# Retention layer of a two-block decoder: the spread of the rotated queries over the heads, from VectorE to ACT

## What is computed

```
x = x + retention(layernorm(x))
def retention(x):
    Q = einsum('bsd,hud->bshu', x, WQ); K = ... WK; V = ... WV
    Q = xpos_rotate(Q); K = xpos_rotate(K)
    QK = einsum('bihd,bjhd->bhij', Q, K)
    scale = 1.0 - 2.0 ** (-5.0 - arange(h))
    R = einsum('bhij,bjhd->bihd', QK * decay_mask(s, scale)[None], V)
    R = group_norm(R, gamma, beta, h)
    return R @ WO
```

## Time and profile before

| what | value |
|---|---|
| median of three runs | 1850.32 us (1847.09 to 1853.89) |
| the profiled execution | 1854.5 us, its span 1852.7 us |
| mean granted TensorE clock | 0.914 of 2.4 GHz |
| TensorE matmuls busy | 1577.7 us, 85% |
| TensorE weight loads busy | 1173.6 us, 63% |
| VectorE busy | 1172.9 us, 63% |
| ACT busy | 714.4 us, 39% |
| POOL busy | 562.4 us, 30% |
| the spread, all layers (L1492) | 640 instructions, 175.6 us |

### The profile page before, as it was taken

One profiled execution on the slowest core, in us unless ns is written; L12 is line 12 of the kernel. 1 busy time (PEld: TensorE's weight loads), 2 busy tenths in 40 slices (PEclk: granted clock), 3 DMA queues, 4 the chain that ended last, 5 costly groups with the idle time before them and its releaser, 6 DMA issues.

```text
span 1852.7 us, 33113 instructions
## 1 busy us (share of the span) xinstructions
PE 1577.7 (85%) x10736; PEld 1173.6 (63%) x10736; DVE 1172.9 (63%) x2970; ACT 714.4 (39%) x1531; POOL 562.4 (30%) x766
## 2 busy tenths in 40 slices
PE   5999949979999999968899995588889999877970
PEld 4655628956666666657799995355556666666850
DVE  5888874357778888775412212677777777775423
ACT  3555555435555555544122220111115555432420
POOL 3111133044443111020133331355551111235526
PEclk9999969989999999959999998798989999776985
DMA  4000000010000000020389894200000000012984
GB/s 170 2 0 0 1 23 23 1 38 10 11 8 4 1 0 0 1 80 1 122 316 328 327 329 167 76 1 0 0 7 13 9 11 9 9 55 86 363 220 136
DMA packets 46683, 137.01 MB, mean 74 GB/s; under 512 B 6445, under 2 KB 29118, under 8 KB 40448
## 3 DMA queue, kind: packets, MB, share of 16 engines
q1 hardware_dynamic: 32288, 110.05, 16.7%
q0 software_dynamic: 7536, 19.67, 3.5%
q10 hardware_dynamic: 6768, 6.16, 1.0%
HBM read 119.21 MB, written 17.56 MB: 74 GB/s over the span
## 4 chain that ended last, share of the span: by engine, by line
PE 57%; DVE 20%; issue 8%; DMA 6%; ACT 4%; POOL 4%; DVEq 1%; ACTq 0%; POOLq 0%; SPq 0%
PE ps L773 9%; PE ps L941 8%; PE ps L818 8%; PE ps L1060 8%; PE ps L851 4%; DVE negmax L1448 4%; PE ps L843 4%; PE ps L1072 4%; DMA back_of<-w_odd 3%; PE ps L866 3%; PE ps L830 2%; DVE probs_all L1456 2%; DVE probsT_all L1443 2%; PE ps L771 2%; PE ps L874 1%
## 5 line engine op out<-in xcount | busy, mean ns | idle before, releaser
L773 PE MATMUL ps<-km,qk 128*128 128x512 f32 x640 | 318.0, 599 | 4.3 <-DVE km L1492 4.3
L1131 ACT ACTIVATE probs_all<-probs_all 128x512 f32<-128x512 f32 x256 | 161.4, 630 | 189.4 <-DVE probs_all L1456 189.4
L1060 PE MATMUL ps<-hT,w_tile 128*128 128x128 f32 x1624 | 203.7, 282 | 3.0 <-DMA w_tile<-in_w_f 2.3
L1448 DVE TENSOR_REDUCE negmax<-ps 128x4 f32<-128x512 f32 x256 | 174.4, 681 | 49.1 <-PE ps L773 48.0
L1060 PEld LDWEIGHTS ps<-hT,w_tile 128*128 128x128 f32 x1624 | 195.6, 198 | 4.4 <-DMA w_tile<-in_w_f 2.5
L638 POOL TENSOR_SCALAR eps_sum<-mv 128x1 f32<-128x1 f32 x112 | 25.0, 223 | 546.0 <-DVE mv L1388 508.0
L1456 DVE TENSOR_TENSOR probs_all<-ps,negmax 128x512 f32<-128x512 f32 x256 | 177.0, 691 | 19.2 <-DVE negmax L1448 1.4
L1492 DVE TENSOR_SCALAR km<-qk,const 128x256 f32<-128x256 f32 x640 | 175.6, 348 | 18.2 <-POOL qk L659 15.6
L773 PEld LDWEIGHTS ps<-km,qk 128*128 128x128 f32 x640 | 119.5, 193 | 83.9 <-issue 73.3
L851 PE MATMUL ps<-const,probs_all 128*128 128x128 f32 x1024 | 160.8, 280 | 12.7 <-ACT probs_all L1131 12.4
L1124 ACT ACTIVATE probsT_all<-ps 128x512 f32<-128x512 f32 x256 | 148.3, 593 | 7.0 <-PE ps L851 6.7
(11 more groups left out here) (240 smaller groups left out, 3104.5 us busy)
## 6 DMA issues: line engine op xcount, KB each, us to landing
w_tile<-in_w_f SPq DMA_DIRECT2D x39, 1536.0 KB, 9.1
w_tile<-in_w_f SPq DMA_DIRECT2D x47, 385.0 KB, 6.1
back_of<-w_odd ACTq DMA_DIRECT2D x47, 128.0 KB
ctxT<-in_ctxT SPq DMA_DIRECT2D x32, 128.0 KB, 2.1
rows_of<-row_of SPq DMA_DIRECT2D x8, 512.0 KB, 3.7
y_back<-back_of SPq DMA_DIRECT2D x8, 512.0 KB, 4.9
w_even<-in_w_att SPq DMA_DIRECT2D x3, 1024.0 KB, 6.9
w_raw<-in_w_f SPq DMA_DIRECT2D x2, 1026.0 KB, 5.5
```

The source lines that it names most:

```text
L773: mm(ps[:, g, :], qk[:, p, stationary + c, :], km[:, c, j:j + HB, :].rearrange("p h k -> p (h k)"), start=mask is None, stop=True).then_in ...
L1060: last = mm(ps[:, 2 * which + at.two, fc * P:(fc + 1) * P], w[:, col:col + P], rowT[:, at.two, c, :], start=c == 0, stop=c == KC - 1)
L1131: nc.scalar.activation(probs[:, g], probs[:, g], ACT.Exp, scale=HD ** -0.5).then_inc(S["probs"], 1)
L1448: nc.vector.tensor_reduce(m, bank, AX.X, ALU.max, negate=True).then_inc(S["dve_sm"], 1)
```

## The change

RET's spread goes to ACT: `spread_queries` issues eight ACTIVATEs (`copy` with a scale: Identity, scale = column j of the head mask, bias 0) into the same `km`, waits for the same POOL semaphore and the same scores, and increments the same km_sb. It is called for `at[1]` ahead of the late `turn_out(at[-1])` and of `weighed(now)`. VectorE's `keys` returns at once for a tile of RET; its wait for POOL stays for the other layer with a rotation.

```diff
--- before.py
+++ after.py
@@ -1173,6 +1173,14 @@
                         last = copy(qk[:, p, m], ps[:, B_QK, m * P:(m + 1) * P], None, vec(names[m // KC], m % KC))
                 last.then_inc(S["qk_sb"], 1)
 
+            def spread_queries(tile):
+
+                wait(act, "pool_m", tile, 3)
+                wait(act, "scores_out", tile.back(1))
+                for j in range(HC):
+                    last = copy(km[:, :, j, :], qk[:, tile.p, 0:KC], head_mask[:, j:j + 1])
+                last.then_inc(S["km_sb"], 1)
+
             def turned_probs(tile, g):
                 if tile.l != RET:
                     last = tile.back(1)
@@ -1209,6 +1217,8 @@
                     exp_zero_keys(now)
                     turned_probs(now, 2)
                     turned_probs(now, 3)
+                if 1 in at and at[1].l == RET:
+                    spread_queries(at[1])
                 if late:
                     turn_out(at[-1])
                 if now:
@@ -1483,11 +1493,13 @@
 
             def keys(tile):
 
+                if tile.l == RET:
+                    return
                 if tile.l in ROTARY:
                     wait(dve, "pool_m", tile, 3)
                 wait(dve, "qk_sb", tile)
                 wait(dve, "scores_out", tile.back(1))
-                src = qk[:, tile.p, 0:KC] if tile.l == RET else qk[:, tile.p, KC:2 * KC]
+                src = qk[:, tile.p, KC:2 * KC]
                 for j in range(HC):
                     last = ts(km[:, :, j, :], src, head_mask[:, j:j + 1], None, ALU.mult)
                 last.then_inc(S["km_sb"], 1)
```

## The result

The changed kernel takes 1916.8 us (median of 4 runs, 1911.6 to 1919.9), the kernel before 1850.7 (4 runs); the ratio is 1.0358, 95% interval 1.0336 to 1.0380. That is 66 us more, where 60 were forecast. The profiled execution took 1918.0 us (span 1916.0) against 1854.5 (1852.7), 63.3 us of span.

A forecast was written before the change was run, and what follows sets the result against it. The order of waits on a loop through TensorE, VectorE and ACT's oT was taken to bind, no engine being full. Delay 52.6, clock 6.5, filling 1 and relief 0 made 60 us on 1850.3: 1910 us, range 1890 to 1932.

The forecast's parts named there:

- The loop and the place of oT: Retention steps: ACT's turned output oT is on the loop that sets the step; VectorE's spread is off it.
- The price of the run: ACT's eight ACTIVATEs: 0.513 us each, starts 0.40 us apart, 3.2 us until ACT's next instruction.
- The cheap end: Rival on ACT: scale operand costs nothing or starts lie 0.26 to 0.31 us apart; 1888 to 1900 us, chance 0.15.
- The delay: ACT's queue: oT waits behind POOL's rotation and the run, 3.76 us later in each of 14 steps, 52.6 us.
- The clock: TensorE's longer wait makes every step a long one: 4 x 1.62 = 6.5 us more.
- The dear case: Rival on TensorE: the 1.2 GHz level covers most of what follows the longer wait; 1926 to 1934 us, chance 0.17.
- Filling: First tiles of retention, filling and draining: ACT's longer run costs 1 us, between 0 and 4.
- VectorE's relief: Taking 2.19 us a step off VectorE is worth nothing; rival that VectorE binds: 31 us gain, 1819 us, chance 0.03.
- The median: Whole kernel: 60 us on top of the median of 1850.3, so 1910 us.
- The other signs: Profile after: steps near 17.8 us, VectorE idle some 6.4 us more, ACTIVATEs 0.40 apart, out projection's wait near 4.7.

The follow-up runs named there:

- filled kernels: TensorE's waits in a retention step filled with unread matmuls: changed kernel (3 and 20) 1892.7 us, ratio 1.0237; kernel before (3 and 3) 1834.4 us, ratio 0.9926.
- one ACTIVATE: Changed kernel, but from the second retention tile ACT issues only one of the eight spreading ACTIVATEs, in the same place: 1867.0 us, ratio 1.0085.
- with four: Changed kernel, but ACT spreads four heads ahead of the turned output and VectorE the other four where it used to: 1897.1 us, ratio 1.0268.
- with sixteen: Changed kernel, but ACT issues eight more ACTIVATEs of the same shape into an unused buffer ahead of the eight: 1966.6 us, ratio 1.0631.
- the loop cut to 11.74 us: Kernel before, spread on VectorE, waits filled with 1 and 3 matmuls, POOL's product with the sines waiting for the head norm: 1822.8 us, ratio 0.9856.

## Why the prediction was right, point by point

**The loop and the place of oT.** Right. Moving the run behind oT brings the time back to within 2 us of the kernel before (ratio 1.0013), with the same work on the same engines.

**The price of the run.** Right: 3.30 us for eight, 3.33 by the spacing of 0.402 and a last one of 0.513; one alone 0.51. The cheap end, starts 0.31 us apart without a price for the scale operand, is refuted by all runs with the spread on ACT.

**The delay.** Right: 14 x 3.76 = 52.6 us against 52.7 with the clock held full in both kernels. TensorE's wait ahead of the out projection was forecast at 4.7 us and is 4.7 to 4.8. That the two meet so closely is partly luck: behind the transposes the out projection starts 3.81 us later in a middle step (5.23 against 1.42 us, both filled), since ACT began 0.13 us behind POOL's sum and not 0.04, and some 0.06 us came back elsewhere in the step.

**The clock.** The term that was mis-sized. I had put every step at the cost of a long one, 1.62 us, 6.5 us on top of the 16 that the kernel before already pays. The filled kernels show 28.5 us, 2.04 a step, 12.1 on top. The step that failed is taking the low stretch to be no more costly behind a longer wait: before, it caught part of the out projection and of the projection in a long step; now it catches the whole out projection in every step. The dear case (3.4 us a step) was too dear. Its course is not simple: 1.17 us a step in the kernel before, 1.12 with one ACTIVATE, 2.38 with four, 2.04 with eight, 1.95 with sixteen (each the 14 steps less 173.7 us and less the delay, 0.402 us for each ACTIVATE and 0.54). The traces show where it lies: from the start of the out projection to the start of the turned sums TensorE takes 2.75 us at a full clock (all 14 steps of both filled kernels), and over the 14 steps it takes longer than that by 16.4 us in the kernel before, 15.1 with one ACTIVATE, 32.5 with four, 28.4 with eight and 28.0 with sixteen. With four, 12 of the 14 take 5.1 to 5.3 us there; with eight they vary from 4.2 to 5.3. Why the low level lasts just so long in each kernel stays open.

**Filling.** +1 was forecast, -0.7 measured: the first scores did start later, by 0.5 us, but took 5.40 us in place of 6.64, since more of them ran at the full clock (0.68 granted in the mean, 0.55 before).

**VectorE's relief.** Worth nothing, as forecast: shown by itself (0.9993) and with the spread last on ACT (0.9998). The Trainium skill's page Perfetto Trace Analysis, section Identifying the Most-Contended Engine, would have one relieve the engine of highest occupancy; no run at the kernel's own loop agrees with 31 us for that. Even where VectorE's queue had come to bind, with the loop cut to 11.74 us, taking half of the spread off it won 0.03 us in a middle step.

**The median.** 1910 us was forecast and 1916.8 measured. The 14 steps make 5.7 us of the miss (64.8 against 59.1), nearly all of it the clock's. By the median the change costs 66 us, by the profiled executions 63, as that of before lies 4 us above its median and that of after 1 us.

**The other signs.** The steps take 18.2 us in place of 17.8, and VectorE is idle 6.9 us more a step in place of 6.4; the spacing (0.40), the wait ahead of the out projection and the wait for the turned sums are as forecast.

## What to carry to other kernels

In a pipeline written out by hand, the place in an engine's queue counts more than the engine: here eight instructions, 3.3 us a step in all, cost 53 us of delay over 14 steps ahead of an instruction on the loop, and next to nothing behind it (ratios 1.0013 and 0.9998). Before work is taken off a busy engine, look who waits for it; if that list is empty, time freed there becomes idle time. The wait that was added on TensorE cost twice here, once as delay (52.7 us) and once in the clock of what followed (12.1 us more), and the second part can be measured by holding the clock full with matmuls that nobody reads.

## What the runs showed of the hardware

- Six matmuls a step of 0.22 us each, without any use, took 16.4 us off the 14 steps of the kernel before (the whole: 1834.4 us, ratio 0.9926): the granted clock of the stretch went from 0.91 to 1.00.
- VectorE's head norm (both inputs in SBUF, 128x256) takes 1.13 us beside POOL's product and 0.39 with POOL made to wait. The Trainium skill's page SBUF — State Buffer, section Who interferes with whom, says that a VectorE instruction with two inputs in SBUF contends with one of GpSimd's that reads SBUF; for the head norm the trace agrees. One wait on POOL for this brought about 9 us (173.7 to 165.0 for the 14 steps).
- An instruction of VectorE on 128x16, with one input in SBUF, takes 0.97 us beside POOL's product with the cosines and 0.17 where it is through before that starts.
